# Value projections on half the columns, and a GpSimd sum ahead of the first combination

## What is computed

```python
# attention, 16 heads of 8 dims, causal softmax
V = proj(Wv, bv)                                   # [4, 16, 512, 8]
y = einsum('bhqk,bhkd->bhqd', softmax(scores), V)  # then @ Wo, gate, residual
# routed FFN: every token is cut into 8 slices of 16 dims, 16 experts, the best two count
h = x @ Wm + bm;  t = h.reshape(-1, 16)
w = softmax(t @ expert_emb);  topw, topi = top_k(w, 2)
hmid = gelu(einsum('td,edi->tei', t, W1) + b1)     # [tokens*8, 16 experts, 64]
eo   = einsum('tei,eio->teo', hmid, W2) + b2
comb = (eo[topi] * topw).sum(over the two)         # weight 0 for the 14 others
out  = comb.reshape(4, 256, 128)-like @ Wo + bo    # gate, residual
```

## Time and profile before

| | us |
|---|---|
| median of 3 runs | 415.25 (414.31 to 416.29) |
| the profiled execution, its own time | 415.93 |
| its span in the trace, first to last instruction | 414.1 |
| PE busy | 354.2 (86%) |
| DVE busy | 286.2 (69%) |
| ACT busy | 257.9 (62%) |
| POOL busy | 110.2 (27%) |
| mean granted TensorE clock | 0.955 of full |

### The profile page before, as it was taken

One profiled execution on the slowest core, in us unless ns is written; L12 is line 12 of the kernel. 1 busy time (PEld: TensorE's weight loads), 2 busy tenths in 40 slices (PEclk: granted clock), 3 DMA queues, 4 the chain that ended last, 5 costly groups with the idle time before them and its releaser, 6 DMA issues.

```text
span 414.1 us, 7342 instructions
## 1 busy us (share of the span) xinstructions
PE 354.2 (86%) x2700; PEld 163.4 (39%) x2700; DVE 286.2 (69%) x595; ACT 257.9 (62%) x300; POOL 110.2 (27%) x159
## 2 busy tenths in 40 slices
PE   3768688897899699998898899998797898879995
PEld 3424254456454334334454434335453223131122
DVE  4769868897879677774869676874759257953333
ACT  9370443344368778665368688655458797948970
POOL 6245306201703024432503034332400032122000
PEclk9968799999699999999899899999999999989999
DMA  7334214100018155520019155531021256605551
GB/s 269 83 69 70 50 30 68 24 5 0 4 36 99 36 139 140 138 57 9 22 38 102 37 136 132 143 55 28 2 44 33 79 136 168 104 1 135 145 142 39
DMA packets 27116, 31.55 MB, mean 76 GB/s; under 512 B 6780, under 2 KB 17788, under 8 KB 27068
## 3 DMA queue, kind: packets, MB, share of 16 engines
q1 hardware_dynamic: 23372, 28.57, 30.4%
q0 software_dynamic: 3456, 2.39, 3.4%
q10 hardware_dynamic: 252, 0.11, 0.2%
HBM read 3.57 MB, written 1.05 MB: 11 GB/s over the span
## 4 chain that ended last, share of the span: by engine, by line
PE 58%; DVE 21%; issue 6%; DMA 5%; ACT 5%; POOL 2%; SPq 1%; POOLq 0%; DVEq 0%; ACTq 0%
PE misc L1269 20%; PE big L1269 18%; PE acc L1269 17%; DVE mx L1014 7%; ACT ring L752 4%; DMA tstack<-tp 4%; PE misc L1291 2%; DVE xn L955 2%; SPq L516 1%; DMA gm<-wT 1%; POOL block L577 1%; DVE gm L1130 1%; POOL rpow L627 1%; DVE stats L930 1%; DVE tf L1068 1%
## 5 line engine op out<-in xcount | busy, mean ns | idle before, releaser
L752 ACT ACTIVATE ring<-big 128x1024 f32<-128x1024 f32 (+2 forms) x225 | 197.6, 928 | 110.7 <-PE big L1269 109.4
L1014 DVE TENSOR_REDUCE mx<-misc 128x1 f32<-128x320 f32 (+7 forms) x157 | 89.1, 590 | 25.0 <-PE misc L1269 23.0
L1269 PE MATMUL acc<-ring,cb 128*32 128x512 f32 x512 | 67.8, 604 | 2.6 <-DVE gm L1130 1.8
L1269 PE MATMUL big<-tstack,w1s 128*128 128x512 bf16 x192 | 56.4, 388 | 9.6 <-DMA tstack<-tp 4.9
L1269 PE MATMUL big<-dense,block 128*128 128x512 bf16 (+7 forms) x256 | 56.1, 325 | 1.8 <-ACT ring L752 1.2
L1130 DVE SCALAR_TENSOR_TENSOR gm<-acc,cb,gm 128x512 f32<-128x512 f32 (+1 forms) x41 | 30.0, 734 | 27.5 <-DMA gm<-wT 17.4
L1269 PE MATMUL misc<-dense,block 128*128 128x256 bf16 (+7 forms) x174 | 43.4, 312 | 4.2 <-DVE mx L1014 2.9
L1269 PE MATMUL acc<-ring,vals 128*32 128x64 f32 (+7 forms) x512 | 43.4, 438 | 0.4
L1269 PEld LDWEIGHTS big<-dense,block 128*128 128x128 bf16 x256 | 31.1, 150 | 25.5 <-ACT ring L752 11.8
L665 POOL TENSOR_TENSOR gm<-osb,gm 128x512 f32<-128x512 f32 x12 | 15.3, 1272 | 95.0 <-ACT osb L792 62.7
L445 POOL DMA_DIRECT2D block<-qk_turned x66 | 39.3, 600 | 1.5 <-issue 1.4
(11 more groups left out here) (161 smaller groups left out, 452.0 us busy)
## 6 DMA issues: line engine op xcount, KB each, us to landing
gm<-wT SPq DMA_DIRECT2D x64, 256.0 KB
dense<-qk SPq DMA_DIRECT2D x42, 64.0 KB
tstack<-tp SPq DMA_DIRECT2D x18, 128.0 KB, 5.1
block<-qk_turned POOLq DMA_DIRECT2D x66, 32.0 KB, 4.0
xs<-in_x SPq DMA_DIRECT2D x4, 256.0 KB, 8.0
ca<-in_pack_a SPq DMA_DIRECT2D x1, 769.0 KB, 7.2
out<-lg SPq DMA_DIRECT2D x3, 256.0 KB, 2.3
dense<-tp SPq DMA_DIRECT2D x6, 128.0 KB, 8.8
```

The lines of the kernel that those rows point to most:

```text
L752: act.activation(dst, src, func, scale=scale).then_inc(s["ring_read"], 1)
L1014: dve.tensor_reduce(mx[:, g, k:k + n, blk], src, AX.X, ALU.max).then_inc(s["misc_read"], 1)
L1269: return pe.matmul(dst, lhsT, rhs, start=start, stop=stop)
```

## The change

1. `values` takes one use `v` instead of `v0`, `v1`. The columns of `wv` are reordered at launch so that those of the even heads come first; PE streams 64 columns for each (block, half) instead of 128: still 16 products, each of half the width. DVE makes two additions of 64x512 instead of four of 64x256.
2. `combine(0)` is four products, not eight: POOL adds slice 4 + h to slice h ahead of it (`sum_halves`, in place, heads 0 and 1 after its slice 7, heads 2 and 3 after its slice 9; for batch 3 all four at the end of its list), and PE waits for the fourth sum of the batch (new semaphore `summed`). POOL waits for each of its sums before it goes on.
3. `CB0_AT` goes from 12 to 14, in the stages of batches 0, 1 and 3. `late` keeps 15.
4. The lists of bank uses get true running numbers (`MISC_START`), since their length is now odd. This changes which bank a use has, not the rule.

```diff
-CB0_AT = HALVES // 2 + 4
+CB0_AT = HALVES - 2
@@ POOL, experts_out
                     k_blocks(b + 2, blocks[:2])
                     del blocks[:2]
+                    if n in (7, 9):
+                        sum_halves(b, range(n - 7, n - 5))
...
+            def sum_halves(b, heads):
+                for h in heads:
+                    wait_weighted(pool, b, 4 + h)
+                    pool.tensor_tensor(gm[:, h, :], gm[:, h, :], gm[:, 4 + h, :], ALU.add).then_inc(s["summed"], 1)
+                    pool.wait_ge(s["summed"], 4 * b + h + 1)
...
             add_bias(("tail", NB - 1))
+            pool.wait_ge(s["x1b_ready"], NB)
+            sum_halves(NB - 1, range(4))
@@ DVE, values
-                for k in range(2):
-                    ...  # per unit v{k}: two tensor_tensor of 64 x (4 blocks x 8 pairs x 8)
+                wait_filled(dve, here, "v")
+                src = bank(here, "v").rearrange("q (s p d) -> q s p d", s=NS, p=NP)
+                for a in range(2):
+                    h = slice(BLK * a, BLK * a + BLK)
+                    dst = vals[h, :, :, (HS + 1) * a:(HS + 1) * a + HS]
+                    ins = dve.tensor_tensor(dst.rearrange("q p s d -> q s p d"), src[h],
+                                            bv[h, :, a, :].unsqueeze(1).to_broadcast([BLK, NS, NP, HS]), ALU.add)
+                ins.then_inc(s["misc_read"], 1)
@@ PE, values
+                wait_bank_free(pe, here, "v")
+                half = D // 2
+                for blk in range(NS):
+                    for a in range(2):
+                        ins = matmul(bank(here, "v")[BLK * a:BLK * a + BLK, half * blk:half * blk + half],
+                                     hT[:, BLK * blk:BLK * blk + BLK], A["wv"][:, half * a:half * a + half])
+                filled(ins)
@@ PE, combine
+                if k == 0:
+                    pe.wait_ge(s["summed"], 4 * here[1] + 4)
+                    for h in range(4):
+                        ins = matmul(dst[HR * h:HR * h + HR, :], B["sum"], gm[:, h, :])
+                    filled(ins)
+                    return
@@ lay_out
-        "wv": np.asarray(i["L0_attn_Wv"]).T,
+        "wv": np.asarray(i["L0_attn_Wv"]).T.reshape(D, NP, 2, HS).transpose(0, 2, 1, 3).reshape(D, D),
```

More of the change, by code:

```diff
@@ L165, in ahead @@
         return [("second", use) for use in uses]
-    parts = [PREPARE + ["v0", "v1"] + ahead(PREPARE), ALONE]
+    parts = [PREPARE + ["v"] + ahead(PREPARE), ALONE]
     parts += [[use if phase == "first" else (phase, use) for uses in WOVEN.values() for phase, use in uses]]
-    parts[2] += ahead(["v0", "v1", ("oT", 0), ("oT", 1)])
+    parts[2] += ahead(["v", ("oT", 0), ("oT", 1)])
     parts += [ahead(LEFT[:-2]), ahead(LEFT[-2:])]
@@ L185 @@
 OPENING, OPENING_BANK, OPENING_PREVIOUS, LAST_IN_ACC = opening()
[L186 to L199, removed]
+MIDDLE = ["yT", "ao"] + PREPARE + ["x1T", "tT", "lg", ("oT", 0), "wT", ("oT", 1), "v"]
+for t in range(2, HALVES + 2):
+    MIDDLE += ["cb0"] * (t == CB0_AT) + CHUNKS[t]
+MIDDLE += ["cb1", "fo"]
+MISC = {("first", 0): OPENING, ("loop", 0): MIDDLE, ("loop", 1): MIDDLE,
+        ("late", NB - 2): ["yT", "ao", "x1T", "tT", "lg", ("oT", 0), "wT", ("oT", 1)]
+        + [use if use == "cb0" else ("tail", use) for _, use in sorted((at, use) for use, at in TAIL_AT.items())]
+        + ["cb1", ("tail", "wT"), "fo"],
+        ("last", NB - 1): ["cb0", "cb1", "cb1+", "fo", "fo+"]}
+MISC_START, n = {}, 0
+for phase, uses in MISC.items():
+    MISC_START[phase] = n
+    n += len(uses)
+HOSTS = {"tail": ("late", NB - 2), "second": ("first", 0)}
 SOFT, EXPERT = NG * NU, len(STEPS) * EH
@@ L363, in use_of @@
         def use_of(here, name):
[L364 to L368, removed]
+            if here[0] in HOSTS:
+                host = HOSTS[here[0]]
+                return MISC_START[host] + MISC[host].index((here[0], name))
+            return MISC_START[here] + MISC[here].index(name)
         def bank(here, name):
@@ L642, in fold_experts @@
                 b = here[1]
-                pool.wait_ge(s["misc_read"], b * MISC_N + MISC_START[here[0]] + CREDIT["misc_read"])
+                pool.wait_ge(s["misc_read"], MISC_START[here] + CREDIT["misc_read"])
                 ready = s["expert_gates"]
@@ L994, in values @@
                 wait_softmax_over(dve, b, turn)
-                for k in range(2):
[L996 to L1006, removed]
+                wait_filled(dve, here, "v")
+                src = bank(here, "v").rearrange("q (s p d) -> q s p d", s=NS, p=NP)
+                bv = A["bv"].rearrange("q (p a d) -> q p a d", p=NP, a=2)
+                for a in range(2):
[4 more added lines that the diff above has]
+                ins.then_inc(s["misc_read"], 1)
             def maximum(here, g, u):
@@ L1304, in values @@
             def values(here):
-                for k in range(2):
-                    unit = f"v{k}"
-                    wait_bank_free(pe, here, unit)
-                    for j in range(4):
-                        at = BLK * (4 * k + j)
-                        for a in range(2):
-                            ins = matmul(bank(here, unit)[BLK * a:BLK * a + BLK, D * j:D * j + D], hT[:, at:at + BLK], A["wv"])
-                    filled(ins)
+                wait_bank_free(pe, here, "v")
[5 more added lines that the diff above has]
+                filled(ins)
             def blocks(stack, p, blk):
@@ L1537, in experts @@
                     if t == cb0_at:
-                        for half in range(2):
-                            combine(here, 0, half)
+                        combine(here, 0, 0)
                     if t == CB1_EARLY and not ahead:
```

10 lines of the change are left out of this document (5 added, 5 removed).

## The result

The changed kernel took 409.55 us (median of 6 runs, 408.79 to 411.56) beside 414.37 (6 runs, 413.50 to 416.29): a ratio of 0.9889, 95% interval 0.9855 to 0.9923, or 4.8 us less with 3.2 to 6.0 inside the interval. Forecast were 3.2 us less. The profiled execution took 409.24 (span 407.4). The total hides two errors of opposite sign, each larger than most terms of the sum.

A forecast was written before the change was run, and what follows sets the result against it. PE was taken to bound expert stages 0 and 1, DVE the stage `late`. Terms 1.7 + 0.8 + 0.1 + 0.1 + 0 + 0.86 - 0.4 = 3.2 us, from 415.25 to 412.0 us; range 409.3 to 414.9.

The forecast's parts named there:

- `late` opens: Rival, chance 0.16: in batch 2's stage DVE reaches its last routing part ahead of POOL's product; 2.0 us more, 410.0 us.
- Values, 0.8: Values of batch 1, after softmax 0: 16 products of half the streamed width save 0.8 us of PE, all counting.
- Loads one after another: Values: if weight loads follow one another instead of overlapping, 1.73 us stays and only 0.24 us is saved.
- Opening, 0.1: Program start: second transposition gets a bank read long before, 0.8 to 1.2 us sooner, but query-block DMAs leave 0.1 us.
- Batches 2 and 3, 0.1: After these batches' values PE, 0.8 us earlier, would wait for DVE: 0.05 us gained each, 0.1 in all.
- Combination in stages 0 and 1, 1.7: Expert stages of batches 0 and 1: four combination products instead of eight save 0.86 us of PE each, 1.7 in all.
- so the sums cost nothing there: Expert stages 0 and 1 and the last: POOL's additions finish in time for its next product and PE's wait; 0 us.
- `late`, 0: Batch 2's stage: PE's saving and DVE's 0.68 us against 0.8 lost to POOL's sums; taken as 0, between -0.8 and +2.
- `last`, 0.86: Last stage: four combination products fewer give back 0.86 us, as PE and ACT are in lockstep.
- Clock, -0.4: Low-clock stretch between 102 and 114 us: PE arrives 0.8 us earlier and works at half pace, 0.4 us lost.

## Why the prediction was right in its total, and where it was wrong

The range was 409.3 to 414.9 and the time, 409.55, lies at its low end, below the 411 to 413.2 that had the chance of 0.48 and next to the 410.0 of the rival "`late` opens" (0.16). The low bound does not follow from the terms given for it: that rival with 0.93 for each combination reaches 409.8. That the total fell into the range is luck in good part: 3.2 us were lost in the stages, and `late`, the banks and the clock gave back more than that.

- **Values, 0.8**: right. 1.15 us in the timeline as worked out from half the gates' pace, 0.82 at rden. Loads one after another would have left 0.24 us of gain; the loads are busy 1.01 us in all, not the 1.71 of the figure cited in the prediction, so here the measurement decides against that reading.
- **Behind the values**: missed, 0.56. I followed the changed bank of `uo` in the opening and not the same change of parity for the maxima.
- **Opening, 0.1**: not settled. In the ten traces with the same code there, the shift ahead of batch 1's values (92.00) goes from +0.01 to -0.66 (-0.45 in the changed kernel), with the low stretches of the first 55 us in other places from trace to trace. Two traces that have the values as before give -0.25 and -0.28.
- **Batches 2 and 3, 0.1**: right in kind; the wait of 0.91 became 1.71, and for batch 2 the shift is the same before and behind it (-2.27 and -2.29).
- **Combination in stages 0 and 1, 1.7**: the size per stage was right (0.85 without the hold), the step "so the sums cost nothing there" failed. I asked whether the sums end in time for POOL's next product and PE's wait (they did), not what DVE does while they run. The rule and the row for it (1.68 against 0.69) stood in my own text, used on `late` alone. Cost: 1.58 us a stage, 3.2 in all.
- **`late`, 0**: the two effects were named and mis-sized. The held steps cost 0.57, not 0.8; with 0.78 back from the combination DVE came 0.06 us ahead of POOL's product, not 0.1 behind. So the rival "`late` opens" is what happened, at 2.1 us; of this 0.7 is work of the engines (the difference to the stage without sums), 1.4 is tied to the low stretch at 366.
- **`last`, 0.86**: right; 0.83 (-4.53 to -5.36), and 0.82 to 0.85 in the ten other traces with that combination.
- **Clock, -0.4**: wrong sign. The stretch at 104 to 111 did not stay: the trace gained 0.46 us there, and 1.6 at 203. Mean granted clock was 0.966 against 0.958 over the timed runs, by the slope above 1.0 us gained.

Terms as measured: -1.46 + 0.82 + 0.56 + 2.1 + 0.86 = 2.9 us with `last` as forecast (0.83 as measured makes no difference), of which 1.4 is clock inside `late`. At equal clock the change gave 3.8, uncertain by 0.8, so about 1 us has no sure place; the opening's 0.45 may be part of it. The trace of before can't stand for all its runs: it has the stretch at 203 and the long end, 3.0 us together, and its time, 415.93, is 1.1 above their mean.

## What to carry to other kernels

Before work is moved to GpSimd, list what VectorE runs in the same microseconds: beside GpSimd's sums and products, steps with two inputs in SBUF and casts or copies from SBUF to SBUF waited until the instruction beside them ended. The two steps with PSUM on one side above did not (0.60 and 0.73), nor did a reduction inside SBUF (0.69 at 350.41, beside a sum). Such a hold stands already in the kernel before, at 334.31: a copy of 128x6 that takes 0.17 us at 291.62, with GpSimd idle, took 1.25 beside a product of GpSimd's. Not every record of GpSimd's holds so: beside its power of 128x4 (107.35, 1.04 us) the same copy took 0.17 at 107.92.

```profile
334.26 1.28 POOL L665 TENSOR_TENSOR gm<-yT,gm 128x512 f32<-128x512 f32 x1 [2.64 <-DMA gm<-wT]
334.31 1.25 DVE L923 COPY modb<-mod 128x6 f32<-128x6 f32 x1
```

Put GpSimd's additions where VectorE reads PSUM; two slices of shift were worth 3 us here, by the trace and at equal clock. And where a step is only just late or only just early for such a lock, price both orders: VectorE 0.15 us behind GpSimd's product lost 1 us, 0.06 ahead of it nothing.

## What the runs showed of the hardware that was not expected

- A cast of 32x128 that takes 0.21 us took 1.29 beside a sum, 1.38 beside a fill and 0.60 beside a copy; a subtraction of the same size 1.38, 0.28 and 0.70. The hold lasts until GpSimd's instruction ends, whatever the size of VectorE's.
- The hold works the other way too: GpSimd's 1.28 us product took 1.76 when VectorE's step came 0.06 us ahead.
- In the changed kernel the subtraction started at 170.19 and was held, though the sum's record starts at 171.06 and GpSimd was then issuing transfers. In the kernel before the same subtraction stood beside the same issues (172.47, in 172.15 to 173.34) and took 0.28, as it did with a fill queued behind them. The record of the start of a sum behind a transfer issue may be late, or the lock is taken sooner than the work starts; that stays open.

```profile
172.47 0.28 DVE L1036 TENSOR_TENSOR nm<-nmr,nm 32x128 bf16<-32x128 f32 x1
```

- A stretch of low clock of 3.4 us (202.9 to 206.3) cost 1.6 us between two softmax stages, seen in ten traces, the kernel before among them, and absent in four.
- One PSUM bank use fewer changes, by parity alone, which of two waits each later user meets: 0.56 us here, behind the values of batch 1.
